# Four column groups of 32 queries for the weighed sum of a windowed attention block, and its projection bias added in the MLP

## The reference, cut to what matters

```python
h = _ln(x, ln1_g, ln1_b)
h = jnp.roll(h, (-s, -s), axis=(1, 2))
win = _window_partition(h, w)
qkv = win @ qkv_w + qkv_b
...
attn = jnp.einsum('bnhd,bmhd->bhnm', q, k) * hd ** (-0.5)
attn = attn + bias.transpose(2, 0, 1)[None]
...
attn = jax.nn.softmax(attn.reshape(nB, nh, N, N), axis=-1)
out = jnp.einsum('bhnm,bmhd->bnhd', attn, v).reshape(nB, N, C)
out = out @ proj_w + proj_b
out = _window_reverse(out, w, B, H, W)
out = jnp.roll(out, (s, s), axis=(1, 2))
x = x + out
h2 = _ln(x, ln2_g, ln2_b)
h2 = jax.nn.gelu(h2 @ fc1_w + fc1_b) @ fc2_w + fc2_b
return x + h2
```

## Time and profile before

| | |
|---|---|
| median of 3 runs | 501.47 us (500.04 to 504.29) |
| the profiled execution | 500.17 us, of which the span is 498.4 |
| mean granted clock of TensorE | 0.985 of full speed |
| attention, first scores to last projection | about 31 to 347 us of the span |
| MLP | about 347 us to the end |

### The profile page before, as it was taken

One profiled execution on the slowest core, in us unless ns is written; L12 is line 12 of the kernel. 1 busy time (PEld: TensorE's weight loads), 2 busy tenths in 40 slices (PEclk: granted clock), 3 DMA queues, 4 the chain that ended last, 5 costly groups with the idle time before them and its releaser, 6 DMA issues.

```text
span 498.4 us, 21474 instructions
## 1 busy us (share of the span) xinstructions
PE 436.9 (88%) x9630; PEld 329.1 (66%) x9630; DVE 383.7 (77%) x549; ACT 294.9 (59%) x437; POOL 378.2 (76%) x376
## 2 busy tenths in 40 slices
PE   0665978899999899999999999787999999999995
PEld 0542756687777777777777767675566676667664
DVE  2767697889999999899999989965467766777652
ACT  1233665675765665666657646543777677767761
POOL 2658989988988989989889799730588888888830
PEclk9995999999999999999999999999999999999999
DMA  8300523511411511511111101100011321330333
GB/s 166 68 1 22 130 64 69 122 30 26 118 34 26 125 29 24 130 25 27 41 26 35 35 24 31 39 3 3 3 40 49 87 59 30 87 78 11 87 90 81
DMA packets 9986, 27.10 MB, mean 54 GB/s; under 512 B 3368, under 2 KB 3368, under 8 KB 7976
## 3 DMA queue, kind: packets, MB, share of 16 engines
q1 hardware_dynamic: 9896, 25.74, 22.0%
HBM read 9.21 MB, written 8.39 MB: 35 GB/s over the span
## 4 chain that ended last, share of the span: by engine, by line
PE 71%; DMA 9%; ACT 8%; SPq 4%; issue 4%; DVE 2%; ACTq 0%; DVEq 0%
PE work L697 26%; PE outs L697 17%; PE scores L697 16%; DMA kX<-kT 5%; PE scores L798 5%; ACT kT L610 4%; PE scores L838 4%; SPq L283 3%; DMA params<-in_params 2%; ACT qT L612 2%; PE work L712 2%; DMA x<-in_x 1%; PE outs L826 1%; ACT probsT L645 1%; SPq L275 1%
## 5 line engine op out<-in xcount | busy, mean ns | idle before, releaser
L373 POOL TENSOR_TENSOR probs<-probs,negmax 128x1024 f32<-128x1024 f32 x64 | 123.8, 1934 | 27.2 <-DVE negmax L489 27.1
L339 POOL TENSOR_TENSOR stat_rstd<-stat_var,minus_half 128x8 f32<-128x8 f32 (+1 forms) x62 | 104.9, 1691 | 5.0
L483 DVE TENSOR_TENSOR probs<-scores,bias 128x1024 f32<-128x1024 f32 x64 | 77.9, 1217 | 14.2 <-PE scores L697 14.2
L645 ACT ACTIVATE probsT<-scores 128x1024 f32<-128x1024 f32 x64 | 65.6, 1025 | 28.8 <-PE scores L798 28.8
L344 POOL TENSOR_TENSOR xn<-x,stat_mean 128x256 f32<-128x256 f32 (+1 forms) x91 | 78.1, 876 | 4.1
L697 PE MATMUL outs<-vX,probsT 128*64 128x34 f32 x2048 | 72.2, 225 | 9.4 <-issue 8.3
L489 DVE TENSOR_REDUCE negmax<-probs 128x16 f32<-128x1024 f32 x64 | 78.1, 1220 | 2.2
L697 PEld LDWEIGHTS outs<-vX,probsT 128*64 128x64 f32 x2048 | 65.9, 138 | 19.1 <-issue 19.0
L697 PEld LDWEIGHTS work<-params,probs 128*64 128x64 f32 x2048 | 62.3, 138 | 23.5 <-DVE x L577 20.5
L798 PEld LDWEIGHTS scores<-ident,probs 128*128 128x128 f32 x512 | 55.5, 142 | 28.1 <-issue 24.2
L610 ACT ACTIVATE kT<-work,bqkv 128x512 f32<-128x512 f32 x31 | 21.3, 688 | 86.6 <-PE work L697 86.6
(11 more groups left out here) (61 smaller groups left out, 662.4 us busy)
## 6 DMA issues: line engine op xcount, KB each, us to landing
kX<-kT SPq DMA_DIRECT2D x124, 64.0 KB, 2.0
x<-in_x SPq DMA_DIRECT2D x32, 224.0 KB
out<-x SPq DMA_DIRECT2D x28, 224.0 KB
x<-in_x SPq DMA_DIRECT2D x32, 32.0 KB
out<-x SPq DMA_DIRECT2D x28, 32.0 KB
out<-x SPq DMA_DIRECT2D x16, 56.0 KB
params<-in_params SPq DMA_DIRECT2D x1, 805.5 KB, 12.0
out<-x SPq DMA_DIRECT2D x16, 8.0 KB
```

The source lines that it names most:

```text
L339: nc.gpsimd.tensor_tensor(stat_rstd[:, cols], stat_var[:, cols], minus_half[:, cols], ALU.pow).then_inc(ln_rstd, pieces)
L373: nc.gpsimd.tensor_tensor(e, e, top, ALU.add).then_inc(shifted, 1)
L483: nc.vector.tensor_tensor(e[:, :].rearrange("q (u a m) -> q a u m", u=2, a=2), scores[k].rearrange("q (a u m) -> q a u m", a=2, u=2), b.re ...
L645: nc.scalar.activation(probsT[n % 2][:, :], trans, ACT.Exp)\
```

## The change

Two parts. In `weigh`, each product takes 32 queries instead of 64, so that its weight has 32 columns and its output 32 partitions; the outputs of one head and u now go to the four column positions 0, 32, 64 and 96, and a step has 32 products. The results are the same numbers in the same places. The bias y_bias is no longer added to half rows in steps 3 and 5 of each group; it is added piece by piece, after the projection: pieces 0 to 3 in steps 48 to 51, piece 4 in step 62, and pieces 5 to 31 in DVE's loop of the MLP, behind the sum of the piece before. `sum2` of a piece waits for its bias, and `add_y` doesn't wait for any.

```diff
+Y_BIAS_STEPS = [PAIRS - 2 * STEPS + i for i in range(4)] + [PAIRS - 2]
...
             def sum2(s):
 
                 dve.wait_ge(ln_mean, MEANS + max(s - 3, 0))
+                dve.wait_ge(y_biased, s + 1)
                 row_sum(x[:, s * PIECE:(s + 1) * PIECE], s % PIECES)
 
-            def add_y_bias(g, half):
-
-                dve.wait_ge(ln_centred, PIECES * (g + 1))
-                dst = x[:, g * ROW + half * 2 * PIECE:][:, 0:2 * PIECE].rearrange("q (a f) -> q a f", f=C)
-                nc.vector.tensor_tensor(dst, dst, y_bias[:, :].unsqueeze(1).to_broadcast([P, 2 * WIN, C]),
+            def add_y_bias(s):
+
+                dve.wait_ge(y_added, COUNT["Y", s // PIECES, 1])
+                dst = x[:, s * PIECE:(s + 1) * PIECE].rearrange("q (a f) -> q a f", f=C)
+                nc.vector.tensor_tensor(dst, dst, y_bias[:, :].unsqueeze(1).to_broadcast([P, WIN, C]),
                                         ALU.add).then_inc(y_biased, 1)
 
             def add_y(of, w):
                 dve.wait_ge(work_ready["Y"], COUNT["Y", of, w])
-                dve.wait_ge(y_biased, 2 * (of + 1))
...
                 norm(n)
-                if n < PAIRS and n % STEPS in (3, 5):
-                    add_y_bias(n // STEPS, (n % STEPS - 3) // 2)
+                if n in Y_BIAS_STEPS:
+                    add_y_bias(Y_BIAS_STEPS.index(n))
...
                 if s + 4 < S:
                     sum2(s + 4)
+                if s + 5 < S:
+                    add_y_bias(s + 5)
...
                 for u in range(2):
                     for h in range(HEADS):
-                        for w in range(2):
-                            at = (u * HEADS + h) * P + (w ^ k) * N
+                        for rows in range(0, P, 32):
+                            w = rows // N
+                            at = (u * HEADS + h) * P + (w ^ k) * N + rows % N
                             row = (w * 4 + 2 * k + u) * HEADS + h
-                            out = outs[w * N:(w + 1) * N, u * HEADS * VW:(u + 1) * HEADS * VW]\
+                            out = outs[rows:rows + 32, u * HEADS * VW:(u + 1) * HEADS * VW]\
                                 .rearrange("q (p h d) -> q p h d", p=2, h=HEADS)[:, :, h]
-                            done = mm(out, probsT[n % 2][:, at:at + N], vX[image % 2][:, row, :])
+                            done = mm(out, probsT[n % 2][:, at:at + 32], vX[image % 2][:, row, :])
```

## The result

The changed kernel takes 516.37 us (median of 4 runs, 516.02 to 517.22) against 500.75 before (4 runs, 496.42 to 504.29): the ratio is 1.034, with a 95% interval of 1.028 to 1.041. The forecast was 493.0, the range 483 to 504. So the kernel is slower, and by more than the range allowed. Some executions of a kernel are longer, at a lower granted clock; the ratios and their intervals leave them out, the medians don't.

What follows compares the result with a forecast made beforehand. PE, busy 88%, bounds the kernel, with ScalarE waits in attention's loop. Weighed-sum savings of 9.4 us less 1.0 for a code stop, bias 0, net 8.4: 500.17 to 491.8, plus 1.3 for the median, 493; range 483 to 504.

Steps and rivals of the forecast that it cites:

- I allow one more such stop: 1.0: Attention on PE: 15 more code packets cost one more stop inside a group, 1.0 us off the gain.
- starved by code: Rival, 9%: in scores and weighed sum late code stops PE, 1.0 us each; 9 stops cancel the gain, one an image gives 523.
- The saving of a step: Weighed sum in attention: 63 intervals at 11.5 ns a pair take 0.72 us, saving 0.18 us a step.
- Full feeding: Rival, 22%: the queue feeds the weighed sum at 8 ns a pair throughout, a step saves 0.39 us, 485.5 us in all.
- The bounds 8 and 15: Weighed sum: ns a pair, 8 if four column positions limit it, 15 at the fastest rate a whole group (scores) holds.
- the burst of the earlier trace: First 0.07 us of a scores group: 8 matmuls and 9 loads start, so PE can be fed below 9 ns a pair.
- No gain: Rival, 18%: PE is fed at the scores' 15 ns a pair, weighed sum 0.94 us, 0.03 more a step, 503 us in all.
- a floor per matmul: Rival, 4%: 29 ns is the price of each matmul start, so a weighed sum takes 1.83 us and the kernel 558.
- The bias in the MLP: 27 additions, one a piece, fit DVE's idle time waiting for rstd; a piece stays at 4.52 us, cost 0.
- The contention with POOL: New DVE additions in the MLP meet POOL at shared SBUF interfaces: 8.6 us if unhidden, taken as 0 by the 0.8 slack.
- The bias in attention: Five new additions, four in steps 48 to 51 and one in step 62, fit DVE's idle time and 0.4 slack: nothing.
- More images wait for kX: Scores in attention: as a sign in the profile after, more than 8 of 20 images wait for the kX DMA.

Runs made afterwards that it cites:

- e11: The kernel before with the moved bias alone, its additions for pieces 0 to 3 in steps 19, 27, 35 and 43: 500.98 us, ratio 1.000.
- e2: The kernel before with the moved bias alone, products still of 64 queries: 505.96 us, ratio 1.015.
- e10: The kernel before (64 queries) with keys and queries ahead of the weighed sum in odd steps: 498.75 us, ratio 0.989.
- e15: The kernel before with 32-query products in odd steps alone, and keys and queries ahead of the weighed sum there: 502.17 us, ratio 0.994.
- e5: The kernel before with 32-query products in the odd steps alone, behind the scores: 518.74 us, ratio 1.038.
- e20: The kernel before with 32-query products in all steps, keys and queries ahead of the weighed sum, loads of x groups 4 to 7 in quarters: 508.46 us, ratio 1.014.
- e16: The kernel before with 32 tiny products (128 instructions) more ahead of attention, in PE's idle time: 502.10 us, ratio 1.002.
- e4: The kernel before with 32-query products in the even steps alone, behind V: 507.06 us, ratio 1.015.
- e8: The kernel before with 15 of V's 16 products an image left out: 505.59 us, ratio 1.011.
- e6: The kernel before with eight waits on a long-reached semaphore behind each 64-query product of the weighed sum: 993.86 us.

## Why the prediction was wrong, point by point

- **The step that failed** is "I allow one more such stop: 1.0". It should have been some 22 stops more and 27 us. I multiplied the price of one stop by the growth of the packet count (15 of 76; it became 16), as if each packet ran the same risk. The risk lies in the time that PE needs from one boundary to the next. No two packets of code start less than 3.27 us apart in any of the 20 profiles, and at nearly all stops PE goes on 2.2 to 3.3 us after the start of the one it waits for. In the kernel before, the four images of a group have 401, 401, 514 and 512 instructions in about 9.0 us each, so they ask for a packet in 5.7 and 4.5 us. In the changed one, images without a stop have 529 in 8.41 us and 642 in 8.69, and ask for one in 4.1 and 3.5. That is at the floor of 3.3 to 3.5, and the run of scores and weighed sum is far below it.
- **The rival "starved by code"** was the right mechanism, for the most part in the right place (some stops stand in the projection and in keys and queries), with nearly the right price (1.0 a stop; 27.0 / 22 = 1.2 measured) and the right point of decision (9 stops), and I gave it 9%. The argument against it ("168.5 busy of 180 us leave no room, so the supply has some reserve") showed only that the reserve sufficed for the old demand. What I hadn't looked up is how long a packet takes: that of the earlier trace rows starts at 286.47, and PE goes on at 289.31, 2.8 us later. Held against the 256 instructions in 2.0 us that I had on the page, that would have told.
- **The saving of a step** was mis-sized: 11.5 ns a pair, measured 9, so 0.29 us for each of both steps (8.99 - 8.41 = 0.58) instead of 0.18. "Full feeding" had the better term. The bounds 8 and 15 held, and the burst of the earlier trace rows was the better witness than the middle. The saving is seen in the images that nothing holds up; where scores wait for kX, part of it is lost.
- **No gain, and a floor per matmul:** both refuted by the same rows.
- **The bias in the MLP** was right to the row: 692 ns, 4.52 us a piece, the wait for rstd gone, cost 0. The contention with POOL that the prediction had put there by the Trainium skill (GPSIMD Engine Reference, its specification table) did not show in the MLP: 692 ns beside 683 for the addition of fc2's bias, and POOL beside it on 8 columns. In attention the traces agree with it: the same instruction takes 0.68 us beside POOL's 8 columns (e11), and 1.40 to 2.28 where it starts within an operation of POOL on 512 or 1,024 (e2).
- **The bias in attention** was wrong: "nothing" for the additions in steps 48 to 51, and 5 us measured. I took 682 ns from L588 without asking what POOL would be doing when the new ones start. They take 1.35 to 2.28 us, and the transposes' slack of 0.4 doesn't cover that. The earlier trace rows had the sign, but not the size: L524's 1542 ns are for 1,024 columns, and are the mean of nine at 1,215 ns and seven at 1,719 to 2,370, which started within an operation of POOL. So the 0.32 us over L534 was no price of one addition. I had also placed the sums of pieces 0 to 3 in the last four steps; they stand in steps 52 to 54, just behind the additions. Nothing forced those to stand together: in e11 they are spread over earlier steps.
- **Removing the additions from attention is worth nothing** held (e11: 1.000).
- **More images wait for kX:** right, 11 waits in the stretch instead of 8, 10.6 us instead of 4.2. That is part of what the 16.7 us contain beyond stops and savings. In e10, with keys and queries ahead of the weighed sum, 1.2 us of it are left between 65 and 340 us, where the kernel before has 8.1. The row of the changed kernel:

```profile
PEld scores L702 <- DMA kX<-kT: 10.6, 11, 1.4
```

Open: what exactly sets off a fetch. The traces narrow it: a packet starts at the median 1.1 us after PE passes a boundary in the changed kernel (mostly between 0.2 and 1.8 us after), and in none of the 20 profiles does PE pass the next boundary less than 2.15 us after that start. The two together are the 3.3 to 3.5 us. A rule that I read off the traces and gave in the expectations (a boundary not less than 3.5 us behind the last) orders e15, e5 and e20 rightly, but its sums are low (for e5 18 us against 24.7, for e20 20 against 33.1), and for e16 it said 6.3 where 2.8 came; some boundaries were only 1.9 to 3 us apart, where the packet had started early, from 1.4 us before the boundary ahead of it to 0.6 us behind it. The stops alone don't give the times either: e4 and e5 lost more than their stops less what their products save, by waits for kX in the one and in part by the lower clock in the other. It wasn't tried to add code to the kernel before at the rate of the 32-query products without other cost, since both ways to do so failed; that the column form is innocent rests on the groups without a stop, on the places of all stops, on e16 and on e15 against e5.

## What to carry to other kernels

Splitting products into smaller ones pays in array time and is charged in instructions. Before such a change, divide the undisturbed time of the loop by its instructions in packets of 256, and do the same for its densest run; here hardly anything under some 3.5 us a packet was to be had, and a kernel at 4.5 to 5.7 us had little trouble while one at 3.5 to 4.1 lost more than it had gained. Price an instruction by a row that has the same work on the engines beside it, not only the same shape: the same addition took 0.68 and 2.28 us in the same stage. And look at the order first: keys and queries ahead of the weighed sum gave 1.1%, and the bias additions moved out of four consecutive steps gave back 1.5%, where the faster products gave nothing.

## What the runs showed of the hardware

- Code reaches PE in packets of 16,384 bytes, 256 instructions, and PE stops at their boundaries if the next isn't there: 26 times in the changed kernel, up to 4.6 us. PE passed no boundary less than 2.15 us after the start of the packet behind it, in 20 profiles. The Trainium skill (Runtime: NRT & Kernel Launch, "Instruction fetch mechanics") says that instruction memory is refilled in blocks of 16 KiB and that crossing a boundary is mostly hidden, because instructions are dispatched more slowly than they are filled. The size of the blocks agrees; that it is hidden doesn't, with 30.7 us of stops in this trace.
- Fewer instructions can be slower: e8, with 7 packets less, takes 5 us more than the kernel before, with 9.8 us of stops instead of 3.7 at boundaries that now lie elsewhere.
- A long stop can be followed by the lower clock: behind a stop of 2.6 us in e8 the granted clock was 0.53 from 176.4 to 183.0 us.
- An addition of 128 x 512 on DVE, both operands in SBUF, took 0.68 us beside an operation of POOL on 8 columns (e11). Started within one on 512 or 1,024 columns it ended 0.55 us behind that one's end, and took 1.40 to 2.28 us (e2). In the kernel before, nine additions of 1,024 columns took 1.22 us, and the seven that started so 1.72 to 2.37.
- A wait on a semaphore that was reached long ago costs PE's sequencer about 0.1 us where it stands as an instruction of its own (e6).
- A matmul of 34 columns was issued each 9 ns on four column positions, with its load. The floor of 25 ns a start, which the prediction had cited from the Trainium skill (TensorE: Matmul & The Clock Gate, "Back-to-back issue gap"), isn't seen.
